# Cross attention on one core: three whole-batch operand stacks, one row store per half, and another route for the output tile

## What is computed

```python
q = split_heads(hidden_states @ w_q)                     # [16, 256, 320], 20 heads of 16
k, v = split_heads(text @ w_k), split_heads(text @ w_v)  # 248 text keys
k_ip, v_ip = split_heads(ip_h @ w_k_ip), split_heads(ip_h @ w_v_ip)  # 8 keys
out = sdpa(q, k, v) + sdpa(q, k_ip, v_ip, mask=mask_ip)
return merge_heads(out) @ w_out + b_out + hidden_states
```

## Time and profile before

| | us |
|---|---|
| median of 3 runs (range) | 658.66 (652.2 to 658.9) |
| the profiled execution, its time | 657.42 |
| its span in the profile | 655.6 |
| key scores of batch 0 begin | 213.10 |
| key scores of batch 15 begin | 625.84 |

### The profile page before, as it was taken

How to read it: one execution, slowest core, us unless ns; L and a number is a source line. 1 busy time by engine, 2 the same in 40 slices (tenths; PEclk the granted TensorE clock), 3 DMA queues, 4 the chain that set the end, 5 groups by cost and what they waited for, 6 DMA issues and landing times.

```text
span 655.6 us, 13734 instructions
## 1 busy us (share of the span) xinstructions
PE 523.5 (80%) x4304; PEld 337.8 (52%) x4304; DVE 387.5 (59%) x706; ACT 297.8 (45%) x515; POOL 125.7 (19%) x203
## 2 busy tenths in 40 slices
PE   4969899999977667866878678787787877878686
PEld 3868778887855344433434344343443434434342
DVE  2565443435335476847568576685766857668543
ACT  4442443434411454535446364464644646446372
POOL 4040000000000032121322213222132221322232
PEclk9979899999978587979899798898989979889899
DMA  9987888888786645353453624526445363452411
GB/s 270 289 243 166 296 266 287 266 274 283 253 208 164 148 132 152 79 171 83 143 155 86 181 76 144 162 74 171 103 133 156 86 171 94 135 160 77 129 46 40
DMA packets 96808, 107.36 MB, mean 164 GB/s; under 512 B 20988, under 2 KB 75836, under 8 KB 96784
## 3 DMA queue, kind: packets, MB, share of 16 engines
q1 hardware_dynamic: 96032, 105.99, 55.2%
q0 software_dynamic: 752, 1.07, 1.3%
HBM read 68.85 MB, written 38.17 MB: 163 GB/s over the span
## 4 chain that ended last, share of the span: by engine, by line
PE 38%; SPq 22%; issue 13%; DMA 12%; DVE 10%; POOL 2%; ACT 1%; DVEq 1%; POOLq 0%; ACTq 0%
PE pv L745 9%; DMA k_stack<-k_parts 7%; SPq L286 6%; PE pj L755 5%; SPq L300 5%; SPq L214 5%; PE score_q L675 4%; DVE max_cols L542 3%; PE score_t L728 3%; DMA probs<-in_wv_ip 2%; PE score_t L636 2%; PE score_t L637 2%; PE score_t L638 2%; DMA v_rows<-v_out 2%; SPq L289 2%
## 5 line engine op out<-in xcount | busy, mean ns | idle before, releaser
L542 DVE TENSOR_REDUCE max_cols<-score_q 128x4 fp32r<-128x992 f32 x160 | 189.1, 1182 | 142.3 <-PE score_q L675 140.2
L477 ACT ACTIVATE probs<-score_t 128x512 f32<-128x512 f32 x320 | 173.7, 595 | 161.2 <-PE score_t L728 159.6
L745 PE MATMUL pv<-probs,v_cur 128*32 128x256 f32 x1920 | 140.3, 432 | 0.7 <-ACT probs L477 0.6
L675 PE MATMUL score_q<-k_stack,q_stack 53*128 53x256 f32 x640 | 80.6, 332 | 45.8 <-DMA k_stack<-k_parts 40.0
L728 PE MATMUL score_t<-q_stack,k_stack 55*128 55x256 f32 x640 | 79.3, 328 | 36.9 <-ACT probs L477 20.2
L755 PE MATMUL pj<-wo_sb,o_all 128*128 128x320 f32 x192 | 78.8, 510 | 29.0 <-DVE out_sb L613 18.7
L675 PEld LDWEIGHTS score_q<-k_stack,q_stack 53*128 53x128 f32 x640 | 53.4, 204 | 87.9 <-issue 57.3
L728 PEld LDWEIGHTS score_t<-q_stack,k_stack 55*128 55x128 f32 x640 | 52.5, 200 | 76.9 <-issue 42.2
L745 PEld LDWEIGHTS pv<-probs,v_cur 128*32 128x32 f32 x1920 | 59.6, 121 | 50.2 <-issue 19.5
L386 POOL TENSOR_TENSOR x_all<-x_all,bias_sb 128x640 f32<-128x640 f32 x16 | 24.7, 1544 | 305.1 <-DMA x_all<-in_x 305.1
L392 POOL TENSOR_TENSOR o_turned<-o_turned,inv_cols 128x256 f32<-128x256 f32 x80 | 49.6, 620 | 167.4 <-DVE inv_cols L601 167.4
(11 more groups left out here) (128 smaller groups left out, 644.8 us busy)
## 6 DMA issues: line engine op xcount, KB each, us to landing
q_stack<-q_parts SPq DMA_DIRECT2D x192, 80.0 KB
k_stack<-k_parts SPq DMA_DIRECT2D x192, 80.0 KB
v_rows<-v_out SPq DMA_DIRECT2D x32, 320.0 KB, 2.4
v_cur<-v_rows SPq DMA_DIRECT2D x16, 640.0 KB
o_all<-in_ctxT SPq DMA_DIRECT2D x16, 512.0 KB, 5.7
q_parts<-qk_out SPq DMA_DIRECT2D x32, 256.0 KB, 2.4
k_parts<-qk_out SPq DMA_DIRECT2D x32, 248.0 KB, 4.4
x_all<-in_x SPq DMA_DIRECT2D x16, 320.0 KB, 3.3
```

Of the source, the lines that this page charges most:

```text
L477: nc.scalar.activation(probs[:, slot(u, p), 2 * S * e:2 * S * (e + 1)], score_t[:, 512 * e:512 * e + 512], ACT.Exp, scale=SCALE)\
L542: nc.vector.tensor_reduce(out=max_cols[:, h, :, at:at + 2].rearrange("p t e -> p e t"), in_=both[:, :, :, 0:TEXT], op=ALU.max, axis=AX.X, ...
L675: last = mm(score_bank(first, p, e)[:, t * KEYS:(t + 1) * KEYS], q_cols(u, p, e, PART + MASKS, t * P, P), k_cols(u, p, e, PART + MASKS, 0, ...
L745: last = mm(pv[32 * t:32 * t + 32, at:at + S], values_of(u, kind, 4 * k + t), probs[:, slot(u, 2 * k + t // 2), a:a + S], start=kind != 1, ...
```

## The change

Three stacks in turn in place of two. The third, `stack2`, takes the place of `c_hl`, whose data it overlays. `load_stack` brings a whole batch in 12 DMAs, issued in batch b for batch b + 2; `q_parts` has a new layout, head by head, so that low and high part come in one DMA of 32 partitions. A half's maxima leave in one DMA. The two exponentials of a step become one of 1024 columns, and query scores come directly behind key scores on PE. `finish` is gone: ACT copies `pj` into `out_sb` (`lift`, steps 7 and 0), and Pool adds the residual there (`add_residual`), two batches later than the batch that it normalises. The loop body holds six batches in place of two.

```diff
+        stack2 = sb("stack2", [P, PAIRS * (S + KEYS)], f32r)
+        c_hi = stack2[:, 0:CC * GT].rearrange("p (c n) -> p c n", c=CC)
+        q_stacks = [q_stack[:, 0, :], q_stack[:, 1, :], stack2[:, 0:PAIRS * S]]
...
             def store_rows(b, h):
                 sp.wait_ge(rows_turned, 2 * b + h + 1)
-                for i in range(4):
-                    sp.dma_start(max_rows[h].rearrange("r (t i n) -> i r t n", t=2, i=4)[i],
-                                 row_buf[32 * i:32 * i + 32, h, :].rearrange("r (t n) -> r t n", t=2))\
-                        .then_inc(rows_stored, 16)
+                sp.dma_start(max_rows[h].rearrange("r (t i n) -> i r t n", t=2, i=4),
+                             row_buf[:, h, :].rearrange("p (t n) -> p t n", t=2)).then_inc(rows_stored, 16)
...
             def first_loads():
...
-                load_stack_q(0, 0, 0)
-                load_stack_k(0, 0, 0)
+                load_stack(Turn(0, 0))
+                load_stack(Turn(0, 1))
...
+            def load_stack(t):
+                done = stack_loaded[t.w]
+                qv = q_stacks[t.w].rearrange("p (a n) -> p a n", a=PAIRS).bitcast(f32)
+                kv = k_stacks[t.w].rearrange("p (a n) -> p a n", a=PAIRS).bitcast(f32)
+                q_cols_of = q_parts[:, :, :, bass.ds(t.b * S, S)].rearrange("(a e) s r n -> e (s r) a n", e=2)
+                masks = aux_rows[bass.ds(t.b, 1), :, :].rearrange("a r n -> (a r) n")
                 for e in range(2):
...
+                    at = HEAD * e
+                    sp.dma_start(qv[at:at + DH, :, :], q_cols_of[e, 0:DH]).then_inc(done, 16)
+                    sp.dma_start(qv[at + DH:at + PART, :, :], q_cols_of[e]).then_inc(done, 16)
+                    sp.dma_start(qv[at + PART:at + PART + MASKS, :, :],
+                                 masks.unsqueeze(1).broadcast_to([MASKS, PAIRS, S])).then_inc(done, 16)
+                for j, part in enumerate((0, 1, 0)):
+                    src = k_parts[part, :, bass.ds(t.b * KEYS, KEYS)].rearrange("(a e r) n -> e r a n", e=2, r=DH)
                     for e in range(2):
                         at = HEAD * e + DH * j
-                        sp.dma_start(kv[at:at + DH, :, :], src[e]).then_inc(stack_loaded[u][h], 16)
-
+                        sp.dma_start(kv[at:at + DH, :, :], src[e]).then_inc(done, 16)
...
+            store_rows(0, 1)
+            load_rows(Turn(0, 0), 1)
+            sp.wait_ge(tile_ready, 10 * GROUPS)
+            load_kaux(2)
+            def batch(t):
+                b, u = t.b, t.u
+                if t.there(2):
+                    need(sp, st_ready, PAIRS * b)
+                    load_stack(t.to(2))
+                if t.there(-2):
                     store_out(b - 2)
                 load_residual(b, u)
-                if there(b, 1):
+                if t.there(1):
                     need(sp, pv_ready, QUADS * b)
                     load_values(b + 1, 1 - u)
-                    store_rows(b + 1, 0)
...
+                    for h in range(2):
+                        store_rows(b + 1, h)
+                        load_rows(t.to(1), h)
             def store_out(b):
-                need(sp, out_done, OT * (b + 1))
+                need(sp, out_done, b + 1)
...
+            def add_residual(b, u):
+                pool.wait_ge(out_evac, OT * (b + 1))
+                pool.tensor_tensor(out_sb[:, :, :], out_sb[:, :, :], x_res[:, u, :, :], ALU.add).then_inc(out_done, 1)
+            def normalise(t):
+                b, u = t.b, t.u
+                if t.there(-2):
+                    pool.wait_ge(biased, b - 1)
+                    add_residual(b - 2, u)
                 pool.wait_ge(xr_loaded[u], 8 * (b - u) + 16)
...
+            def lift(b, t):
+                act.wait_ge(out_ready, OT * b + t + 1)
+                if t == 0:
+                    need(act, out_stored, 16 * b)
+                nc.scalar.activation(out_sb[:, t, :], pj[:, 0:D], ACT.Copy).then_inc(out_evac, 1)
...
+                    if t.there():
+                        act.wait_ge(st_ready, PAIRS * b + p + 1)
+                        if p % 2 == 0:
+                            need(act, pv_ready, QUADS * b + (p - 4) // 2 + 1)
+                        nc.scalar.activation(probs[:, slot(u, p), :], score_t[:, :], ACT.Exp, scale=SCALE)\
+                            .then_inc(exp_done, 1)
+                    for k, off in EVACUATE.get(p, ()):
+                        if t.there(off):
+                            evacuate(b + off, (u + off) % 2, k)
+                    for m, off in LIFT.get(p, ()):
+                        if t.there(off):
+                            lift(b + off, m)
...
                 for p in range(PAIRS):
-                    if there(b):
-                        key_scores(b, u, p)
+                    if t.there():
+                        key_scores(t, p)
+                        if t.there(1):
+                            query_scores(t.to(1), p)
                     for k, off in VALUES.get(p, ()):
...
-                    if there(b) and there(b, 1):
-                        query_scores(b + 1, 1 - u, p)
...
-FINISH = {6: [(0, -1)], 0: [(1, -2)]}
+LIFT = {7: [(0, -1)], 0: [(1, -2)]}
```

More of the change, by code:

```diff
@@ L128, in xattn @@
         kaux_stored, kaux_loaded = sem("kaux_stored"), sem("kaux_loaded")
+        kaux2_loaded = sem("kaux2_loaded")
         aux_stored = sem("aux_stored")
-        stack_loaded = [[sem(f"stack_loaded{a}{h}") for h in range(2)] for a in range(2)]
+        stack_loaded = [sem(f"stack_loaded{w}") for w in range(3)]
         v_loaded = [sem("v_loaded0"), sem("v_loaded1")]
@@ L160, in xattn, with __init__, to, there @@
         slot = lambda u, p: (PAIRS * u + p) % 4
-        def there(b, off=0):
-            return not isinstance(b, int) or 0 <= b + off < B
-        def batches(eng, body, tail=True):
-            for u in range(2):
-                body(u, u)
-            with eng.Fori(1, B // 2 - 1) as i:
-                for u in range(2):
-                    body(2 * i + u, u)
-            for b in (B - 2, B - 1):
-                body(b, b % 2)
+        class Turn:
+            def __init__(self, i, c):
+                self.i, self.c, self.b = i, c, 6 * i + c
+                self.u, self.w, self.r = c % 2, c % 3, 2 * i + c // 3
+            def to(self, off):
+                return Turn(self.i, self.c + off)
+            def there(self, off=0):
+                return not isinstance(self.i, int) or 0 <= self.c + off < B
+        def batches(eng, body, tail=True):
+            for c in range(2):
+                body(Turn(0, c))
+            with eng.Fori(0, 2) as i:
+                for c in range(2, 8):
+                    body(Turn(i, c))
+            for c in (B - 2, B - 1):
+                body(Turn(0, c))
             if tail:
-                body(B, 0)
+                body(Turn(0, B))
         def groups(eng, body):
@@ L236, in group @@
                 store_qk(g, 2)
-                if not more:
-                    load_stack_q(0, 0, 1)
                 for t in range(2 * GB):
@@ L243, in group @@
                         .then_inc(v_stored[t % 2], 16)
-                    if t == 1 and not more:
-                        load_stack_k(0, 0, 1)
                 if more:
@@ L251, in group @@
                         store_rows(0, 0)
-                        load_stack_q(1, 1, 0)
-                        load_rows(0, 0, 0)
-                    if not more and j == 4:
-                        load_stack_k(1, 1, 0)
+                        load_rows(Turn(0, 0), 0)
             def first_loads():
@@ L401, in _ @@
             batches(pool, normalise, tail=False)
+            pool.wait_ge(biased, B)
+            for b in (B - 2, B - 1):
+                add_residual(b, b % 2)
         @block.scalar
@@ L672, in query_scores @@
                     need(pe, max_done, n if first else n - 1)
-                for t in range(2):
+                for tile in range(2):
                     for e in range(2):
-                        last = mm(score_bank(first, p, e)[:, t * KEYS:(t + 1) * KEYS],
-                                  q_cols(u, p, e, PART + MASKS, t * P, P),
-                                  k_cols(u, p, e, PART + MASKS, 0, KEYS), start=True, stop=True)
+                        last = mm(score_bank(first, p, e)[:, tile * KEYS:(tile + 1) * KEYS],
+                                  q_cols(w, p, e, PART + MASKS, tile * P, P),
+                                  k_cols(w, p, e, PART + MASKS, 0, KEYS), start=True, stop=True)
                 last.then_inc(sq_ready, 1)
@@ L728, in key_scores @@
                         last = mm(score_t[:, 512 * e + S * tile:512 * e + S * tile + S],
[L729 to L732 removed]
+                                  k_cols(t.w, p, e, PART + MASKS + 2, tile * P, P),
+                                  q_cols(t.w, p, e, PART + MASKS + 2, 0, S), start=True, stop=True)
+                last.then_inc(st_ready, 1)
             def values(b, u, k):
```

137 lines of the change are left out of this document (43 added, 94 removed).

## The result

The changed kernel takes 749.23 us (median of 4 runs, 744.19 to 751.21), the kernel before 655.84 in the same session: a ratio of 1.142, 95% interval 1.132 to 1.151. I had predicted 587 with a range of 566 to 624. The profiled execution took 748.56 with a span of 746.8, against 655.6 before: 91.2 us more.

A forecast was written before the change was run, and what follows sets the result against it. SyncE's issue queue between turned maxima and scores was taken to set 27.5 us a batch; steps on PE and ACT would then set 22.5. 655.6 - 15 x (27.5 - 22.5) + 1 + 4, +1.8 around it: 587 us, range 566 to 624.

The forecast's parts named there:

- The queues behind it: DMAs of a batch, issued in a row: stack pieces drain in 7.6 us, residual seen at 15.3, all just hidden.
- my own round: Turn of step 9 through stack loads, residual and Pool to the next turned maxima: 21.8 us, just under 22.2.
- about 1 us to be seen: Delay after output and residual have moved at 14.3 us until their landing is noticed, giving 15.3.
- (b): Rival: the queue's round decides, through a costlier row store or slower stack burst; +2.9 makes 24.7 a batch, 620 us; chance 0.25.
- (d): Rival: slower than before because the stack burst drains above 105 ns a piece; at 115 ns about 681 us; chance 0.04.
- the lift's wait: At step 7 project_out on PE waits for ACT's copy, with key scores of step 8 queued behind: +1.76 us a batch.
- Ends: Time outside the 15 batch distances: +1 us (0 to +5) before batch 0, +4 in the last batch and tail.
- A steady pair of steps: Two successive steps of the loop without stalls, in the new order on PE and ACT: 4.00 us, before 3.79.
- the merged exponential: One exponential of 1024 columns out of PSUM on ACT: 1.05 us, between 1.00 and 1.15.
- the store with 4 outermost: The single row store runs on 4 DMA engines instead of 16: +0.7 us, or +3.6 at 60 ns a piece.
- What I named as proof of the contrary: Signs of a wrong prediction: turn_back waits for Pool, row stores land late, clock falls after step 7's wait (+1.3 a batch).
- The third sign: Row stores of the maxima landing far later than 3 us would show the prediction wrong.

The follow-up runs named there:

- e13: Transfers only, no attention: one batch's stack loads without masks; kernel before's form 18.2 us, changed kernel's 15.8, interleaved 13.7, six DMAs of 32 partitions 10.6 to 10.9.
- e3: Changed kernel with two output tiles in turn, so the lift waits for the store of two batches before: 729.13 us, ratio 1.118.
- e4: Changed kernel with every HBM row of q_parts and k_parts 4 KB longer: 752.62 us, ratio 1.153.
- e1: Kernel before with only the new head by head layout of q_parts: 690.06 us, ratio 1.056.
- e6: Changed kernel with low and high parts of q and k interleaved row by row in HBM, ten loads per stack: 716.64 us, ratio 1.093.
- e7: e6 with k loads split off behind the first half's rows, and the second stack's first loads moved behind the last group's stores: 655.6 us, ratio 0.997.
- e11: Kernel before with one row store per half and interleaved q and k parts, ten DMAs per half stack instead of 14: 586.09 us, ratio 0.895.

## Why the prediction was wrong

**The step that failed** stands under "The queues behind it": "While k loads run, 0.73 of 16 engines move 199 GB/s, that is 60 ns a piece: 7.6 us". The same burst alone takes 15.8 us (e13), 132 ns for each of 120 pieces per engine. The window 500:503 was one in which SyncE was issuing and the engines were not full; its busy share was no price for a full queue. A window of stage 1, which I had not used, shows it in the trace of before (columns as in the earlier trace rows):

```profile
183.00:186.00 3.00, 1.23 (x9) 0.96 (x7) 0.68 (x1) 0.52 (x2) 0.00 (x0) 1.00 1.09 182
```

It was not that output and residual had been issued inside that window: the two us before, with stack loads alone, give 60 ns as well (117 / 0.43 = 272 GB/s). With the engines partly idle the record has one of them busy for 60 ns with a piece; the full queue of e13 passes one piece per engine in about twice that.

```profile
498.00:500.00 2.00, 1.90 (x30) 0.94 (x28) 0.84 (x3) 1.48 (x3) 0.00 (x0) 1.00 0.43 117
```

With 15.8 in place of 7.6 my own round becomes 21.8 + 8.2 = 30.0 us. That is an upper figure, since 15.8 holds the first start and the last landing, which my sum had apart. The rate inside that burst gives a lower one:

```profile
86.00:99.00 13.00, 0.00 (x0) 1.00 1.11 149
```

1.97 MB at 149 GB/s are 13.2 us or 110 ns a piece, with the masks' pieces 13.9, and the round 28.1. Measured were 30.4 per batch, and 29.4 with the missed wait taken away (e3). So the term was short by 6 to 8 us. (The "about 1 us to be seen" further on in that sum rests on no row.)

The burst's rate is the mechanism of rivals (b) and (d): (b), at 0.25, gave it 2.9 us, and (d), at 0.04, a worst case of 115 ns. The 110 ns lie inside (d)'s band, whose 681 us fell short by the ends (47.7 us where it had 5) and by a batch of 30.4 for its 28.8. The reason by which I all but excluded (d), that whole-batch loads walk the same HBM rows, was beside the point: HBM rows didn't matter (e4), partitions did.

**A wait that I did not see.** The diff shows `need(act, out_stored, 16 * b)` in `lift`, and no step of mine costs it. Before, `finish` needed the same store, but that had landed in 2.8. Behind the burst it lands in 11.7, just when step 7 wants it. Taking it away gives back 20 us of the 91 (e3) and no more, since the two other rings are nearly as long. I priced the lift's wait at 1.76 as a handoff between engines and never asked which transfer it hangs on.

**Ends: +1 and +4, measured +40.4 and +7.3.** Of the 40.4, 27.9 are the layout of `q_parts` (e1, and e6 the other way). I treated it as part of the load, and didn't ask what it does to the store in stage 1. 7.7 are the second stack's twelve loads ahead of the last group's stores (e7 against e6, with the split's own part not taken out). The other 5 I can't assign; the first stack as one piece, which stands in the same place, is the candidate, and the trace shows PE waiting for it: the very first query scores idle 20.9 us for `k_stack`, until 223.95 (11.9 in e6), where in the kernel before no wait for it was longer than 3.9. The tail has the missed wait once more: the store of the last batch but one is issued at 735.49, and ACT, which has to lift into the same tile, idles 5.83 until it has landed. With two output tiles the tail is 34.4 instead of 37.1 (e3).

```profile
223.95 0.80 PE L668 MATMUL score_q<-k_stack,q_stack 53*128 53x256 f32 x4 [20.94 <-DMA k_stack<-k_parts]
...
737.87 0.44 ACT L472 ACTIVATE out_sb<-pj 128x320 f32<-128x320 f32 x1 [5.83 <-DMA out<-out_sb]
```

**Right, as far as it goes.** A steady pair of steps is 4.05 (412.61 to 416.66) for 4.00 predicted; the merged exponential 1022 ns for 1.05; the batch without a burst 21.3 us for 22.2. Row store to row loads takes 2.3 us (409.79 to 412.13) against about 1.8 from the last of the four stores before, so the store with 4 outermost costs about 0.5; I had 0.7. The steps were the part that I worked on longest, and the bound lay elsewhere.

**What I named as proof of the contrary came in:** `turn_back` waits for Pool (19.2 in all, and 96.2 in e3), and the clock falls in the stall, with the values at 2.41. The third sign came in for one half: the row store of the first half, behind the burst, is issued at 422.68, and the row loads that wait for it go out at 434.15, 11.5 us later; that of the second half takes 2.3.

```profile
422.68 0.56 SPq L223 DMA_DIRECT2D max_rows<-row_buf  x1
...
434.15 0.57 SPq L229 DMA_DIRECT2D q_stack<-max_rows  x2
```

**The gain that was there.** The single row store in the old kernel gives 3.1 us a batch, where I had expected 625 to 635 us and got 609.1. The granted clock rises with it, from 0.911 to 0.952, and how much of the 3.1 comes from that was not separated.

## What to carry to other kernels

Price a transfer from a window in which the DMA engines are full, and by the number of partitions that it reaches: a busy share below 1 times a rate is not a capacity. When many loads are gathered ahead of a store or a load that something waits for, work out when that one lands, and list every semaphore that hangs on it. A new layout of an intermediate tensor is paid on both sides, so cost the store as well as the load, and try the small parts of a large change alone: here one store in place of four, with wider stack loads, made the kernel 10% faster (e11), and the whole change made it 14% slower.

## What was not expected of the hardware

- Loads of 1.97 MB from HBM in pieces of 1 KB, issued back to back: 18.5 to 19.3 us on 16 partitions per DMA (102 to 106 GB/s), 11.0 on 32, 13.3 to 14.8 on 48, where a DMA takes twice as long as one on 32 (3.07 us against 1.53); 2.10 MB on 128 partitions took 8.4. Pieces of 10 KB on 16 partitions: 17.9 to 18.3.
- On 32 partitions it made no difference whether they began at 0 or at 16, nor which of three layouts they came from (10.6 to 10.9).
- The DMA share reads 1.10 to 1.17 while the engines move as little as 98 to 175 GB/s. The same kind of loads moved 117 GB/s at a share of 0.43.
- A store with 8 or 4 outermost in HBM, in pieces of 2 KB, lengthened stage 1 by 28 us (e1), while one of 256 pieces of 128 B with 4 outermost cost about 0.5 us.
